# A Mamba-2 block and a Hadamard FFN on one core: the decays' differences split between ScalarE and GpSimd, and the sums of dt one weight tile later

## The reference

```python
zxbcdt = einsum('bld,de->ble', xn, w_in)             # z, xBC and dt
dt = softplus(dt + dt_bias);  A = -exp(A_log)
xBC = silu(causal_conv4(xBC) + conv_b)               # then split into xh, B, C
cs = cumsum(dt * A)                                  # inside a chunk
Lmat = exp(cs[l] - cs[s]) for s <= l                 # the decays
Y_diag = sum_s (C[l] . B[s]) * Lmat[l, s] * xh[s] * dt[s]
Y_off = exp(cs[l]) * C[l] . state                    # state: carried from chunk to chunk
y = (Y_diag + Y_off + D * xh) * silu(z)
out = (y / rms(y) * norm_w) @ w_out
```

## Time and profile before

| | |
|---|---|
| median of 3 runs | 981.42 us (979.32 to 981.63) |
| profiled execution, its own time | 977.44 us |
| its span in the profile | 975.6 us |
| PE busy | 941.0 us, 96% |
| DVE busy | 577.1 us, 59% |
| ACT busy | 353.4 us, 36% |
| POOL busy | 331.7 us, 34% |

### The profile page before, as it was taken

The page is one execution under the profiler, slowest core; times in us unless marked ns, Lnnn a source line. Parts: engine busy times, 40 slices in busy tenths (PEclk is TensorE's granted clock), DMA queues, the critical chain, the costliest instruction groups (busy, mean ns, idle before and its releaser), DMA issues.

```text
span 975.6 us, 13290 instructions
## 1 busy us (share of the span) xinstructions
PE 941.0 (96%) x5000; PEld 471.2 (48%) x5000; DVE 577.1 (59%) x955; ACT 353.4 (36%) x546; POOL 331.7 (34%) x370
## 2 busy tenths in 40 slices
PE   9899878998899999999999999999999999999998
PEld 4344444544444445555454445555455445555543
DVE  7876678775633766576442766576442756575521
ACT  6778755523323334222222334232221433232200
POOL 0000655562000206585210205676310204766410
PEclk9999998999999999999999999999999999999999
DMA  9798252643223435435223435445222434255122
GB/s 338 245 329 290 104 183 83 226 145 113 93 98 111 149 100 162 144 94 173 86 67 107 144 97 163 136 112 158 86 81 89 152 98 163 65 152 151 44 76 97
DMA packets 76206, 134.25 MB, mean 138 GB/s; under 512 B 7536, under 2 KB 20464, under 8 KB 74096
## 3 DMA queue, kind: packets, MB, share of 16 engines
q1 hardware_dynamic: 56640, 104.88, 33.4%
q10 hardware_dynamic: 19504, 28.53, 9.5%
HBM read 107.43 MB, written 25.95 MB: 137 GB/s over the span
## 4 chain that ended last, share of the span: by engine, by line
PE 65%; POOL 3%; DMA 2%; DVE 1%; issue 0%; DVEq 0%; ACT 0%; POOLq 0%
PE ps L594 43%; PE ps L828 14%; PE ps L790 2%; DMA arena<-cs_rows 2%; PE ps L782 2%; PE ps L776 1%; PE ps L762 1%; POOL arena L1447 1%; POOL arena L1433 1%; POOL arena L1437 0%; POOL arena L1443 0%; PE ps L613 0%; PE ps L632 0%; PE ps L745 0%; PE ps L765 0%; POOL arena L1423 0%
## 5 line engine op out<-in xcount | busy, mean ns | idle before, releaser
L594 PE MATMUL ps<-xh,arena 128*128 128x512 f16 x1592 | 490.8, 382 | 1.1 <-DVE arena L1174 0.9
L594 PE MATMUL ps<-xl,arena 128*128 128x512 f16 x796 | 303.7, 382 | 0.0
L594 PEld LDWEIGHTS ps<-xh,arena 128*128 128x128 f16 x1592 | 159.1, 100 | 190.0 <-issue 10.1
L828 PE MATMUL ps<-arena 128*128 128x512 f16 x768 | 171.1, 379 | 0.0
L1423 POOL TENSOR_TENSOR arena<-arena 128x512 f16<-128x512 f32 x64 | 82.0, 1285 | 220.7 <-ACT arena L972 220.7
L1433 POOL TENSOR_TENSOR arena<-arena 128x2048 f32<-128x2048 f32 x16 | 58.8, 3677 | 207.5 <-DMA arena<-cs_rows 207.5
L1224 DVE SCALAR_TENSOR_TENSOR arena<-ps,cw,arena 128x511 f32<-128x511 f32 (+2 forms) x120 | 89.5, 748 | 63.3 <-ACT arena L962 61.5
L594 PEld LDWEIGHTS ps<-xl,arena 128*128 128x128 f16 x796 | 78.2, 98 | 89.8 <-issue 5.0
L828 PEld LDWEIGHTS ps<-arena 128*128 128x128 f16 x768 | 74.2, 98 | 91.0 <-issue 5.5
L972 ACT ACTIVATE arena<-arena 128x512 f16<-128x512 f32 x64 | 40.3, 629 | 171.3 <-DVE arena L1245 171.3
L1240 DVE SCALAR_TENSOR_TENSOR arena<-arena,ps 128x512 f32<-128x512 f32 x64 | 43.9, 685 | 67.4 <-ACT arena L967 64.7
(11 more groups left out here) (178 smaller groups left out, 1092.3 us busy)
## 6 DMA issues: line engine op xcount, KB each, us to landing
arena<-w_parts SPq DMA_DIRECT2D x198, 256.0 KB, 2.6
w_parts<-arena SPq DMA_DIRECT2D x66, 256.0 KB, 2.4
arena<-cs_rows ACTq DMA_DIRECT2D x16, 1024.0 KB, 6.2
...
```

What stands on the lines that cost most here:

```text
L594: ins = nc.tensor.matmul(out_ap, lhs(i, a), rhs(i, c), start=(i == 0 and s == 0), stop=(i == n - 1 and s == 2))
L828: ins = nc.tensor.matmul(bank(t), hw[a][:, i, t * P:(t + 1) * P], w2s[i % W2R][:, d, :], start=(i == 0 and s == 0), stop=(i == JF - 1 and ...
```

## The change

Four edits, with the bodies of the old E moved into a new item ES. Heads 0 to 7 of `Eb` are made on ACT: eight instructions, one a head, that compute relu(cs[s] - cs[l]), that is the negative of the capped difference; the Exp of this half has scale -1. Heads 8 to 15 stay on POOL with the two old instructions at half their size, and `pool_mark` goes. ACT's eight are in two items of four (ES with an even and an odd number), POOL's two in the even one. E keeps only the DMAs, which now wait for both halves of the chunk before. In `STEP_FIRST` E stands two tiles earlier. In `FIRST`, SUM stands behind C4.

```diff
-FIRST = ("B G1S C C0 G1N C1 Z0 DT C2 DTL Z1 C3 Z2 SUM C4 Z3 WOL F0 C5 ...
+FIRST = ("B G1S C C0 G1N C1 Z0 DT C2 DTL Z1 C3 Z2 C4 SUM Z3 WOL F0 C5 ...
-FRONT = "CZCCZCZCZCZCPCZCZCPZ"
+FRONT = "CZCCZCZeCZCZeCPCZCZCPZ"
-STEP_FIRST = {... "E": (None, 10, 18, 26),
+STEP_FIRST = {... "E": (None, 8, 16, 24),
+ES_FIRST = (3, 4, 11, 13, 19, 21, 28, 30)
+ES_AT = (None,) * 2 + (7, 9, 15, 16, 24, 26)
...
+            elif f == "e":
+                seq.append(("ES", sum(k == "ES" for k, _ in seq)))
...
+    steps += [(at, len(STEP_AT) + 1, ("ES", i)) for i, at in enumerate(ES_AT if b else ES_FIRST) if at is not None]
...
                         act.wait_ge(esub_ok.sem, esub_ok.at(b, c - 1))
+                        act.wait_ge(emin_ok.sem, emin_ok.at(b, c - 1))
                         act.dma_start(csbc.rearrange("p h l -> p (h l)"),
...
+                    elif kind == "ES":
+                        c, part = divmod(i, 2)
+                        if part == 0:
+                            act.wait_ge(d_csbc, (b * NC + (c + 1)) * 16)
+                            act.wait_ge(sums_ok.sem, sums_ok.at(b, 0))
+                            act.wait_ge(pe_diag.sem, pe_diag.at(b, c - 1))
+                        for h in range(part * NH // 4, (part + 1) * NH // 4):
+                            ins = nc.scalar.activation(Eb[:, h, :], csbc[:, h, :], ACT.Relu, scale=-1.0,
+                                                       bias=cs_s[:, c * NH + h:c * NH + h + 1])
+                        if part == 1:
+                            ins.then_inc(esub_ok.sem, 1)
...
                     elif kind == "X":
+                        act.wait_ge(esub_ok.sem, esub_ok.at(b, c))
+                        nc.scalar.activation(Eb[:, 0:NH // 2, :], Eb[:, 0:NH // 2, :], ACT.Exp, scale=-1.0)
                         act.wait_ge(emin_ok.sem, emin_ok.at(b, c))
-                        nc.scalar.activation(Eb, Eb, ACT.Exp).then_inc(eexp_ok.sem, 1)
+                        nc.scalar.activation(Eb[:, NH // 2:, :], Eb[:, NH // 2:, :], ACT.Exp).then_inc(eexp_ok.sem, 1)
...
-                    elif kind == "E":
+                    elif kind == "ES" and i % 2 == 0:
+                        c = i // 2
...
-                        nc.gpsimd.tensor_tensor(Eb, csbc, cs_s[:, c * NH:(c + 1) * NH].unsqueeze(2).to_broadcast([P, NH, P]),
-                                                ALU.subtract).then_inc(esub_ok.sem, 1)
-                        pool.wait_ge(esub_ok.sem, esub_ok.at(b, c))
-                        nc.gpsimd.tensor_tensor(pool_mark[:], ones[:, 0:1], ones[:, 0:1], ALU.mult)
-                        nc.gpsimd.tensor_scalar(Eb, Eb, 0.0, -3.0e38, ALU.min, ALU.max).then_inc(emin_ok.sem, 1)
+                        half_of = Eb[:, NH // 2:, :]
+                        nc.gpsimd.tensor_tensor(half_of, csbc[:, NH // 2:, :],
+                                                cs_s[:, c * NH + NH // 2:(c + 1) * NH].unsqueeze(2).to_broadcast([P, NH // 2, P]),
+                                                ALU.subtract).then_inc(eneg_ok.sem, 1)
+                        pool.wait_ge(eneg_ok.sem, eneg_ok.at(b, c))
+                        nc.gpsimd.tensor_scalar(half_of, half_of, 0.0, -3.0e38, ALU.min, ALU.max).then_inc(emin_ok.sem, 1)
```

More of the change, by code:

```diff
@@ L39 @@
 WARM = (32, 8)
-FIRST = ("B G1S C C0 G1N C1 Z0 DT C2 DTL Z1 C3 Z2 SUM C4 Z3 WOL F0 C5 F1 SQ0 Z4 F2 C6 F3 QS0 Z5 F4 C7 F5 SQ1 Z6 F6 Z7 F7 QS1 E0 A0").split()
-FRONT = "CZCCZCZCZCZCPCZCZCPZ"
+FIRST = ("B G1S C C0 G1N C1 Z0 DT C2 DTL Z1 C3 Z2 C4 SUM Z3 WOL F0 C5 F1 SQ0 Z4 F2 C6 F3 QS0 Z5 F4 C7 F5 SQ1 Z6 F6 Z7 F7 QS1 E0 A0").split()
+FRONT = "CZCCZCZeCZCZeCPCZCZCPZ"
 FIRST_AT = ([("WOQ", q, q + 1) for q in range(8)] + [("WOS", 0, 10)] +
@@ L417, in build @@
         esub_ok = signal("esub_ok", NC, 1)
[L418 removed]
+        eneg_ok = signal("eneg_ok", NC)
+        emin_ok = signal("emin_ok", NC, 1)
         eexp_ok = signal("eexp_ok", NC)
```

5 lines of the change are left out of this document (2 added, 3 removed).

## The result

The changed kernel took 966.87 us (median of 4, 965.39 to 969.27), the kernel before 980.37 us beside it (4 runs, 977.97 to 981.63). The ratio is 0.987, 95% interval 0.984 to 0.990: faster by 13.5 us. A second timing (e10) gave 0.988 (0.984 to 0.992). The forecast was 975.0 us, range 969.0 to 980.5.

A forecast was written before the change was run, and what follows sets the result against it. PE, busy 941.0 of 975.6 us, bounds batches 1 to 3; batch 0 is a chain over all engines. Batch 0's -4.5 and the fourth term's -1.9 make -6.4 us: 971.0 profiled, 975.0 on the median, range 969.0 to 980.5.

The forecast's parts named there:

- First term: Front of batch 0: with SUM behind C4, PE works through its wait for `av`; F0 starts 1.3 us earlier.
- Price of the work: On ACT a Relu takes 0.3 us, four 1.2, a chunk 2.4, all 38; splitting the Exp adds about 0.1 per chunk.
- Rival C: Slower: ACT's queue becomes batch 0's bound if no Relu is covered; +5.6 us, 987.0 us, chance 0.10.
- Second and third term: Batch 0, chunks 0 and 1: no `Xdec` wait, shorter QS5 wait; -2.0 us at QS4 including the first term, then -1.8.
- rival B: Batch 0's long waits vanish together with the 1.2 GHz clock behind them; -10 to -14 us, 969.5 us, chance 0.15.
- For the rest of batch 0 I take -0.1: Batch 0 behind W0: E3's wait for t1 is covered by DVE's own list; only -0.1 us gained.
- DVE's operations stand less behind GpSimd's: Chunk 0 of batch 0: DVE's operations with two SBUF inputs wait less for GpSimd, so `Xdt` comes earlier.
- Fourth term: Chunk 2 of batches 2 and 3: PE's waits of 1.40 and 1.0 us for `Xdec` go; -1.9 us gained.
- The base: Whole kernel: profiled execution 977.44 us gives 971.0; the median shown, 981.42, is 4 us above, so 975.0.

The follow-up runs named there:

- e10: The changed kernel again, unedited, timed and profiled a second time; ratio 0.988 to the kernel before.
- e15: The changed kernel with 4 heads on ACT and 12 on GpSimd, the Exp cut at the fourth head; ratio 0.9876 to the kernel before.
- e9: The changed kernel with each of ACT's Relus cut into four over 32 columns; ratio 1.0185 to the kernel before.
- e3: The changed kernel with all 16 heads made on GpSimd and one Exp, keeping only the new places and SUM behind C4; ratio 0.9924 to the kernel before.
- e14: The kernel before, unedited, profiled a second time; its profiled execution took 975.03 us.
- e4: The kernel before with matmuls of no use under five PE waits in batch 0 (SUM, S0, QS5, W0, H0); ratio 0.9948 to the kernel before.
- e7: e2 with 12 matmuls of no use under PE's wait ahead of SUM; ratio 0.9897 to the kernel before, 3.7 us faster than e2.
- e12: The kernel before with 12 matmuls of no use under its wait ahead of SUM alone; ratio 1.0000 to the kernel before.
- e2: The changed kernel with SUM back ahead of C4; ratio 0.9935 to the kernel before.
- e1: The kernel before with one edit, SUM behind C4; ratio 0.9988 to the kernel before.
- e17: e1 with GpSimd's L1433 as four instructions over 512 columns in place of one over 2048; ratio 0.9942 to the kernel before.
- e6: The changed kernel with each of GpSimd's two instructions of the differences done twice, ACT's half kept; ratio 0.9929 to the kernel before.

## Why the prediction was wrong

**First term, -1.3.** Right in size: F0 came 1.4 us earlier (1.0 to 1.5 over the three profiles), and C4 took PE's place at 45.08 where 45.1 was forecast. Of its two legs only ACT's was right. PE's 8.6 us from SUM to F0 had the stretch at 1.2 GHz in it; without it PE was through early and stood 1.60 us ahead of F0 at 53.73, and the copy of ACT that L876 was (L882 now) ended at 53.63 and gave the time.

**Price of the work.** Right: four Relus in 1.28 us where 1.2 was forecast, mean 389 ns; two Exps of 1045 ns, 0.1 us more than one of 1.89 by the overlap. Whether ACT makes 4 heads or 8 can't be told in the timing (e15), and nearly three times the work costs 30 us (e9). In the profiles a little is paid already: from L782 of chunk 2 to H0 of batch 0 it is 28.9 us with 8 heads on ACT, 28.3 with 4 (e15), 27.8 with none (e3, where GpSimd makes all), and 34.2 in e9. Rival C had a true mechanism and the wrong size.

**Second and third term.** The mechanisms were right: no wait for `Xdec` was left, and QS5's went altogether. The sizes were fair beside the first profile of the kernel before (QS4 -2.9, -2.4 and -1.2 for -2.0; QS5 -5.4, -3.3 and -3.7 for -3.8) and too small beside the mean of its two: 3.5 us at QS4, 5.5 at QS5 and 6.8 at W0, where -4.4 was forecast. e14, which makes that difference, has twice the stretch at 1.2 GHz behind SUM (6.8 us), and its F0 is 0.9 us late already. Which of the two profiles is the kernel's can't be said from two.

**No term for the clock.** This is the step that failed most. The sum priced every wait by its length and gave matmul time nothing; the slow clock is named behind two of the waits, and counted in rival B alone, as something that goes only if three waits go whole, with a chance of 0.15. What the runs showed: PE's busy time fell by 6.3 us in the first pair of profiles, 6.1 of them by the clock, and by 2.9 over the five. The time at 1.2 GHz fell from 23 to 12 us over the timed executions, an estimate of 3 us by their own scatter. e4 and e7 give 4 to 5 us for covering the stops of kernels with 20 us at 1.2 GHz. The waits that rival B wanted gone (`av`, `Xdec`, QS5) did go, and its 969.5 us came nearest of the four times that the prediction gives, though with new stops at C4, QS4 and Y1, which it did not have. That the gain comes in steps, because removing one stop frees nothing while the next is there, fits e12 and the table of the parts, but is argued and not shown.

**"For the rest of batch 0 I take -0.1"** failed too. From L782 of chunk 2 to H0 the kernel before took 30.4 and 29.7 us (e14), the changed kernel 28.9 in all three profiles: 0.8 to 1.4 us, which I had passed over. It is not the split's alone. e2, with the split and the places, has 28.9 and e1 30.4, but e3, with the places and no split, has 27.8, and e17, with only GpSimd's instruction cut, 28.5. What these share is that DVE meets GpSimd's long instruction less; that it is the cause here was not tested. The other 1.7 us that the first profile gained behind H0 are the stretch from 225.1 to 228.5. They belong to the execution and not to the change: e14 didn't have it either, and e10 did, at 218.2.

**No term for DVE's other stands.** I counted "DVE's operations stand less behind GpSimd's" only at the two places shown. e17 shows that this alone, without any split, is worth 4.5 us, with what the clock then gives back; by e3 and e6 some 5 of the 12 us hang on GpSimd's time. These numbers and the clock's overlap and must not be added.

**Fourth term, -1.9.** The mean is about right (batches 1 to 3 shrank by 2.3 us over the three profiles after and by 0.6 over the two before: 1.7), and that is in part luck. The wait of 1.40 us is made by a row of cs that landed 8.7 us behind its issue; in e1, with the same code there, the row came 6.5 us behind and L782 of that chunk didn't wait. The term priced one execution's landing as if it were the kernel's. What the change gives is that a late row no longer matters: the wait appears in both profiles of the kernel before, and in none of the three of the changed one, though its rows in this chunk came 8.0 to 8.9 us behind their issue.

**The base.** The profiles' mean gain is 8.7 us, the timings' 12 to 13. The profiled executions of the kernel before, 977.44 and 975.03 us, lie below its medians (978 to 980), those of the changed kernel (965.39, 968.65, 968.56) about at its own. The remaining 3 to 4 us are in executions that no trace shows. Their clocks are on record, and settle a part: the kernel before has 23 us at 1.2 GHz on average and some 20 in the two profiled ones, which by the 0.29 of above is 1 us. Later rows of cs would do the rest; that was not seen and stays open. Open too is why the clock fell behind H0's wait of 2.31 us in e2 and e10 and not in the first profile, with the same wait, nor behind 3.46 us in e14.
